# A four-stage attention and state-space model on one core: one activation table set, earlier reciprocals, moved norm products, and a two-lane final norm

## The chip, the cores and the metric

The kernel runs on one core of one Trainium2 chip. The metric is the device time of one execution in microseconds (us), lower is better. All data is float32.

## The reference, cut to what matters

The input is `x` of shape (8, 512, 256) and a context of shape (8, 64, 192). Four parts run one after the other, each adding to `x`:

```
L0: x += SelfAttn(LN(x));  x += CrossAttn(LN(x), ctx);  x += W2 (u * gelu(v)) with u, v = LN(x) Wp     (16 heads of 64)
L1: 64 context tokens in front of x, 4 mamba layers, each h += mamba(rmsnorm(h)); then rmsnorm(h); the 64 tokens dropped
L2: x += CrossAttn(LN(x), LN(ctx));  x += W2 gelu(LN(x) W1)                                            (16 heads of 16)
L3: x += one-head cross-attention with LN on both sides
LN(x) = (x - mean) * rsqrt(var + 1e-5) * g + b;      rmsnorm(x) = x * rsqrt(mean(x*x) + 1e-5) * w
attn = softmax(q k^T * scale) v
```

## The kernel before, in words

The kernel is written by hand, engine by engine. Each stage is a block with one instruction stream for each engine; semaphores order them, and a barrier stands between stages. `x` stays in SBUF as `X`, with the 256 features on partitions (two halves, KD = 2) and tokens along the free axis, so that the mean over features is a matmul with a matrix of 1/256. PSUM has 8 banks; bank 6 is `lane_v` (emptied by VectorE, the page's DVE), bank 7 is `lane_s` (emptied by ScalarE, ACT). The stages are self-attention, the first cross-attention, a gated feed-forward, a small prepend stage, mamba, `final_norm`, the second cross-attention (behind a norm of the context), a second feed-forward, and the last attention. Each loops over the 8 batches, and within batch b it prepares the norm of batch b+1.

**A layer norm** has these steps: TensorE (PE) makes the mean (L157), DVE subtracts it (`norm_centre_dve`, L174), ACT squares (L190), PE makes the variance in `lane_s` (`norm_variance_pe`, L166), ACT takes Ln in place (L197) and Exp with scale -0.5 (L199, which frees `lane_s`), together the reciprocal root (`norm_root_act`), DVE scales (L182) and ACT adds the bias (L206). ACT looks a function up in a table set; where the set held does not serve the function, the build puts an ACT_TABLE_LOAD in front. Before, Ln and Exp are served by two different sets.

**Self-attention** goes over 16 steps h; a step is a pair of heads with half of the queries, so two steps make one pair. A step has two units (u = 0, 1), each one tile of 128 queries for both heads. For each unit PE makes scores in two banks (L343), DVE takes the row maxima (L406), ACT exponentiates with row sums (L466), DVE inverts the sums (L412), POOL (GpSimd) multiplies the probabilities (L496), PE transposes them two steps later (L334, g = h - 2) into banks 4 and 5, which DVE (L401) and ACT (L458) copy out. These banks are single: the transposes of a unit wait for the copies of the unit before, the first half for DVE's, the second for ACT's. After every second step PE makes the output product (L360). The order in each stream is by hand: PE does transposes of (g,0), scores of (h,0), transposes of (g,1), scores of (h,1); DVE does copy (g,u), maximum (h,u), reciprocal (h-1,u); ACT does the copies of (g,0) and (g,1), then the exponentials of (h,0) and (h,1). The reciprocal is thus two units behind the maximum. Batches 0 to 6 carry the next batch's norm in this loop: PE's mean behind step g = 4, its variance behind g = 8, ACT's root (L478, L480) behind g = 9, DVE's scaling behind g = 10 and ACT's bias behind g = 12.

**Cross-attention** (`cross_attention`, used twice) goes over QT = 4 query tiles: PE makes the scores i = 0 to 3 (L676; from i = 2 on after DVE's subtraction i - 2 is done), then for t = 0 to 3 the transposes (L693), with the output projection of the batch before (`project_out`, L653, two parts) ahead of t = 0 and t = 2, then the mixing product (L703). `project_out` waits until both lanes are free. DVE does maximum (L765), subtraction (L767), sum (L774) and reciprocal (L776) of each tile, and POOL the multiplication (L621). The norm of the next batch stands in between: PE's mean behind score tile 1, its variance behind score tile 3; DVE's centring behind the sum of tile 0; ACT's squares behind exponential 2 and the root behind exponential 3.

**final_norm** (from L2078) is a loop over 8 batches with one lane: ACT squares, PE makes the mean square, ACT takes Sqrt, DVE a reciprocal over 512 columns (L2105) and two products (L2109).

## Time and profile before

| | us |
|---|---|
| median of 3 runs | 7805.58 (7801.66 to 7806.82) |
| the profiled execution's own time | 7797.73 |
| its span | 7795.7 |
| busy PE / DVE / ACT / POOL | 6613.3 / 5299.9 / 3872.3 / 4707.4 |

In the timeline a line is a run of like instructions: start, length, engine, source line, and in square brackets the idle time of that engine before it with what ended it. PEclk is the granted TensorE clock as a share of 2.4 GHz. A fp32 matmul or transposition stands as one or two instructions; "x16" counts instructions.

### The profile page before, as it was taken

Reading aid. Unit: us, or ns where it says so; the run is one execution under the profiler, and the core shown is the slowest. Engines: PE = TensorE matmul, PEld = TensorE weight load, DVE = VectorE, ACT = ScalarE, POOL = GpSimd, SP = SyncE. Lnnn points to the kernel's source line nnn. Section 1 sums busy time; section 2 is a strip of 40 time slices with the busy share of each in tenths; the row PEclk is TensorE's granted clock in tenths of the full one; section 3 lists DMA queues with packets and bytes.
Section 4 is the critical chain, followed back from the end, with each engine's and each line's share of the span. In section 5 each row is a group of like instructions: output and inputs, shape, how many; then the busy total and the mean of one; then the engine's idle time right before and its main releaser. Section 6 shows DMA issues by size and latency. Waiting matters only on the chain. (4 is left out here: it accounts for less than half of the span.)

```text
span 7795.7 us, 74709 instructions
## 1 busy us (share of the span) xinstructions
PE 6613.3 (85%) x20398; PEld 2699.1 (35%) x20398; DVE 5299.9 (68%) x6209; ACT 3872.3 (50%) x6998; POOL 4707.4 (60%) x2266
## 2 busy tenths in 40 slices
PE   7889898888898888888888888888888888777887
PEld 3444344444443323322333322332233332233333
DVE  3444444433321699999999999999999999755222
ACT  4444444322222566666666656666666666532332
POOL 2333333210000699999999999999999999611000
PEclk9999999988999999989999989999999998878998
DMA  1000000000000323323323332332332332300000
GB/s 65 0 0 0 0 0 0 17 0 0 15 0 2 78 61 83 76 70 87 80 69 70 90 75 69 82 77 61 93 80 61 84 79 68 85 5 0 0 0 22
DMA packets 205932, 351.49 MB, mean 45 GB/s; under 512 B 34112, under 2 KB 43008, under 8 KB 205360
## 3 DMA queue, kind: packets, MB, share of 16 engines
q1 hardware_dynamic: 205616, 347.96, 18.7%
q8 instruction: 115, 1.88, 0.1%
q14 instruction: 201, 1.65, 0.1%
HBM read 189.18 MB, written 6.62 MB: 25 GB/s over the span
## 5 line engine op out<-in xcount | busy, mean ns | idle before, releaser
L2046 POOL TENSOR_TENSOR work<-work,weights 128x1024 f32<-128x1024 f32 x1152 | 2691.4, 2361 | 19.1 <-DMA weights<-mamba_bc 12.8
L1903 PE MATMUL banks<-work 128*64 128x512 f32 x4608 | 1378.3, 680 | 629.0 <-POOL work L2051 615.6
L1965 DVE TENSOR_TENSOR_SCAN banks<-banks,work 128x512 f32<-128x512 f32 x1296 | 1617.7, 1270 | 70.8 <-ACT banks L2012 66.9
L2012 ACT ACTIVATE banks<-work 128x512 f32<-128x512 f32 x2304 | 1497.6, 680 | 67.0 <-DVE work L1729 43.2
L1965 DVE TENSOR_TENSOR_SCAN work<-banks,work 128x512 f32<-128x512 f32 x1008 | 1264.6, 1269 | 126.1 <-ACT banks L2012 79.4
L2051 POOL TENSOR_TENSOR work<-work,weights 128x1024 f32<-128x1024 f32 x504 | 1187.7, 2356 | 87.6 <-ACT work L1621 87.6
L1467 PE MATMUL banks<-work,weights 128*128 128x512 f32 (+31 forms) x3796 | 1164.1, 457 | 5.3 <-DVE work L1702 3.0
L496 POOL TENSOR_TENSOR work<-work 128x1024 f32<-128x1024 f32 x256 | 483.8, 1892 | 939.5 <-DVE work L412 939.5
L1467 PEld LDWEIGHTS banks<-work,weights 128*128 128x128 f32 x3796 | 643.8, 192 | 623.1 <-issue 543.7
L1747 DVE TENSOR_TENSOR work<-banks,weights 128x512 f32<-128x512 f32 x1296 | 852.8, 669 | 0.0
L1903 PEld LDWEIGHTS banks<-work 128*64 128x64 f32 x4608 | 267.0, 145 | 1502.8 <-POOL work L2051 920.5
L1625 ACT ACTIVATE work<-banks 128x2 f32<-128x2 f32 x648 | 111.4, 172 | 1217.6 <-DVE work L1747 1210.1
L406 DVE TENSOR_REDUCE work<-banks 128x2 f32<-128x1024 f32 x256 | 312.5, 1223 | 165.6 <-PE banks L343 165.4
L621 POOL TENSOR_TENSOR work<-work 128x1024 f32<-128x1024 f32 x64 | 121.0, 1900 | 440.1 <-DVE work L776 440.1
L466 ACT ACTIVATE work<-banks,work 128x512 f32<-128x512 f32 x512 | 346.1, 683 | 77.2 <-DVE work L406 77.2
L334 PE MATMUL banks<-ident,work 128*128 128x128 f32 x2048 | 284.9, 282 | 96.4 <-POOL work L496 81.2
L1485 PE MATMUL banks<-work,weights 128*128 128x512 f32 x592 | 351.3, 723 | 0.0
L889 PE MATMUL banks<-work,weights 128*128 128x512 f32 x768 | 341.8, 599 | 11.0 <-ACT work L206 11.0
L334 PEld LDWEIGHTS banks<-ident,work 128*128 128x128 f32 x2048 | 222.9, 142 | 290.1 <-POOL work L496 230.0
L343 PE MATMUL banks<-work 64*128 64x512 f32 x1024 | 294.2, 656 | 22.0 <-ACT work L466 16.4
L1050 POOL TENSOR_TENSOR work<-work,one 128x64 f32<-128x64 f32 (+1 forms) x16 | 4.3, 289 | 503.1 <-SPq L1044 312.7
L458 ACT ACTIVATE work<-banks 128x512 f32<-128x512 f32 x256 | 152.7, 596 | 237.3 <-PE banks L334 236.2
(218 smaller groups left out, 8418.8 us busy)
## 6 DMA issues: line engine op xcount, KB each, us to landing
weights<-mamba_bc SPq DMA_DIRECT2D x592, 256.0 KB, 5.0
work<-work SPq DMA_DIRECT2D x1160, 128.0 KB, 2.3
weights<-in_in_w SPq DMA_DIRECT2D x10, 512.0 KB, 4.1
weights<-in_conv_rows SPq DMA_DIRECT2D x20, 256.0 KB, 4.7
X<-in_xT SPq DMA_DIRECT2D x2, 2048.0 KB, 11.5
out_T<-X SPq DMA_DIRECT2D x2, 2048.0 KB, 9.7
weights<-in_out_w SPq DMA_DIRECT2D x5, 512.0 KB, 4.0
mamba_bc<-work SPq DMA_DIRECT2D x37, 64.0 KB, 1.6
```

The lines of the kernel that those rows point to most:

```text
L334: mm = e.transpose(core.banks[:, 4 + j, kt * P:(kt + 1) * P], probs[:, 2 * (g % 2) + u, j, kt * P:(kt + 1) * P], core.ident[:])
L466: last = e.activation(probs[:, slot, j, :], core.banks[:, 2 * u + j, :], ACT.Exp, bias=nmax[:, slot, j:j + 1], accum_out=sums[:, slot, j:j ...
L496: e.tensor_tensor(probs[:, slot], probs[:, slot], rsum[:, slot, :].unsqueeze(2).to_broadcast([P, 2, T]), ALU.mult) \
L889: mm = e.matmul(bank(i), w1[:, k, m * P:(m + 1) * P], normed[:, k, :], start=(k == 0), stop=(k == KD - 1))
L1467: mm = e.matmul(lane[:, a:b], conv_w[j][:, k, m * P:(m + 1) * P], nb[:, k, a + j:b + j], start=(d == 0 and k == 0), stop=(j == 0 and b == ...
L1485: mm = e.matmul(lane, z_w[:, k, m * P:(m + 1) * P], nb[:, k, TAPS - 1:], start=(k == 0), stop=(k == KD - 1))
L1747: last = e.tensor_tensor(ring_pair(n, j)[:, h, :], banks[:, slot_of(i), :], bc[:, j % SP_, 1, :], ALU.mult)
L1903: mm = e.matmul(ybank[k % 2][64 * h:64 * h + 64, :], fold, ring_pair(n, j)[:, h, :], start=False, stop=(a == SP_ - 1))
L1965: e.tensor_tensor_scan(ub if by_pool(j) else da, da, ub, state[:, i:i + 1], ALU.mult, ALU.add).then_inc(scanned, 1)
L2012: e.activation(banks[:, slot_of(i), :], dt_rep[:, k % 2, h, :], ACT.Exp, scale=decay[:, f:f + 1]).then_inc(da_full, 1)
L2046: e.tensor_tensor(ring_pair(n, j), u_rep[:, k % 2], bc[:, a, 0, :].unsqueeze(1).to_broadcast([P, 2, TC]), ALU.mult) \
L2051: e.tensor_tensor(ring_pair(n, q), ring_pair(n, q), bc[:, q % SP_, 1, :].unsqueeze(1).to_broadcast([P, 2, TC]), ALU.mult) \
```

## The change: what it does, and the diff

Five things. (1) At the start of ACT's stream in six stages and in the norm of the context, and before the root in the feed-forwards, the table set `natural_log_exp_and_others`, which holds both Ln and Exp, is loaded. (2) In self-attention DVE takes the reciprocal of the unit directly before the one whose maximum it has just made. (3) In the cross-attentions the mean and the centring go one tile forward, the squares go behind exponential 1, PE's variance goes behind the transposes of t = 0, and ACT's root behind the copy of t = 0. (4) `final_norm` uses the two lanes in turn and two buffers of squares, and takes Ln and Exp on ACT in place of Sqrt and DVE's reciprocal. (5) Its loops are written out.

```
@@ self_attention, vector
-                        if 0 < h <= H0:
-                            n = b * (H0 * UNITS) + ((h - 1) * UNITS + u)
-                            slot = 2 * ((h - 1) % 2) + u
-                            e.wait_ge(exp_done, n + 1)
+                        m = h * UNITS + u - 1
+                        if 0 <= m < H0 * UNITS:
+                            slot = m % (2 * UNITS)
+                            e.wait_ge(exp_done, b * (H0 * UNITS) + (m + 1))
                             e.reciprocal(rsum[:, slot, :], sums[:, slot, :]).then_inc(rsum_ready, 1)
@@ scalar, at the start: self_attention, norm_context, cross_attention, feed_forward, last_attention
+            e.preload_act_table_set("natural_log_exp_and_others")
@@ cross_attention, tensor
-                    if more and i == 1:
+                    if more and i == 0:
                         norm_mean_pe(e, core, ln, V, x_in(b + 1), core.mean_d, T)
-                    if more and i == 3:
-                        norm_variance_pe(e, core, nm, ln, S, b + 1, x_in(b + 1), core.mean_d, squared, T)
                 for t in range(QT):
...
                     mm.then_inc(t_full, 1)
+                    if more and t == 0:
+                        norm_variance_pe(e, core, nm, ln, S, b + 1, x_in(b + 1), core.mean_d, squared, T)
@@ cross_attention, vector
-                    if more and i == 1:
+                    if more and i == 0:
                         norm_centre_dve(e, core, ln, V, x_in(b + 1), centred, T)
@@ cross_attention, scalar
-                    if more and i == 2:
+                    if more and i == 1:
                         norm_square_act(e, nm, ln, v_done(b), rows, centred, squared)
-                    if more and i == 3:
-                        norm_root_act(e, core, nm, ln, S, b + 1, std, T)
                 for t in range(QT):
...
+                    if more and t == 0:
+                        norm_root_act(e, core, nm, ln, S, b + 1, std, T)
@@ feed_forward, scalar
                     if more and i == VARIANCE_AT:
+                        e.preload_act_table_set("natural_log_exp_and_others")
                         norm_root_act(e, core, nm, ln, S, b + 1, std, T)
@@ final_norm
+    squared, _ = core.area(0, 2, KD, T)
+    lane = lambda b: (core.lane_v, core.lane_s)[b % 2]
...
         @block.tensor
-            with e.Fori(0, B) as b:
+            for b in range(B):
                 e.wait_ge(squared_ready, b + 1)
-                e.wait_ge(s_free, b)
+                if b >= 2:
+                    e.wait_ge(scaled, b - 1)
                 for k in range(KD):
+                    mm = e.matmul(lane(b), core.mean_d[:], squared[:, b % 2, k, :], start=(k == 0), stop=(k == KD - 1))
...
         @block.scalar
+            e.preload_act_table_set("natural_log_exp_and_others")
+            for b in range(2):
+                e.activation(squared[:, b], x_in(b), ACT.Square).then_inc(squared_ready, 1)
+            for b in range(B):
+                e.wait_ge(full, b + 1)
+                e.activation(lane(b), lane(b), ACT.Ln, bias=core.eps[:]).then_inc(logged, 1)
+                if b + 2 < B:
+                    e.activation(squared[:, b % 2], x_in(b + 2), ACT.Square).then_inc(squared_ready, 1)
+                e.wait_ge(logged, b + 1)
+                e.activation(lane(b), lane(b), ACT.Exp, scale=-0.5).then_inc(rooted, 1)
...
         @block.vector
-                e.reciprocal(std, std).then_inc(inverted, 1)
+            for b in range(B):
+                e.wait_ge(rooted, b + 1)
                 for k in range(KD):
+                    last = e.scalar_tensor_tensor(out=x, in0=x, scalar=core.v("final", k), in1=lane(b), op0=ALU.mult, op1=ALU.mult)
                 last.then_inc(scaled, 1)
```

## Rows read from the trace of the kernel before

**Rows 1.** Windows: us, then each engine's busy time (instructions), PEclk, DMA share, GB/s
```profile
56.00:1447.00 1391.00, 1245.42 (x5157) 568.91 (x5155) 607.51 (x938) 621.92 (x1462) 483.84 (x256) 0.99 0.00 0
...
1447.00:2086.00 639.00, 558.64 (x1792) 292.79 (x1792) 239.65 (x300) 140.50 (x192) 69.53 (x67) 0.85 0.01 5
```

**Rows 2.** Groups of instructions on ACT: busy us, mean ns, idle before
```profile
L199 ACT ACT_TABLE_LOAD x43 | 55.2, 1283 | 0.8
...
L1688 ACT ACTIVATE banks<-banks,eps 128x512 f32<-128x512 f32 x38 | 25.2, 662 | 35.1 <-PE banks L1493 35.1
```

**Rows 3.** Timeline of two steps of self-attention: start us, us, engine, line
```profile
288.13 1.09 PE L334 MATMUL banks<-ident,work 128*128 128x128 f32 x8
...
293.07 0.21 ACT L466 ACTIVATION_READ_ACCUMULATOR work<-banks,work 128x1 f32 x1
...
293.66 1.09 PE L334 MATMUL banks<-ident,work 128*128 128x128 f32 x8 [1.29 <-POOL work L496]
...
295.01 0.59 ACT L458 ACTIVATE work<-banks 128x512 f32<-128x512 f32 x1
...
296.76 1.13 PE L343 MATMUL banks<-work 64*128 64x512 f32 x4
...
301.41 1.09 PE L334 MATMUL banks<-ident,work 128*128 128x128 f32 x8
```

**Rows 4.** Timeline of the two steps after the next batch's root
```profile
346.07 0.66 PE L334 MATMUL banks<-ident,work 128*128 128x128 f32 x4 [0.88 <-ACT work L458]
...
351.18 1.07 PE L334 MATMUL banks<-ident,work 128*128 128x128 f32 x8 [1.04 <-POOL work L496]
```

**Rows 5.** Timeline of the last batch of self-attention, first transposes
```profile
1327.05 1.09 PE L334 MATMUL banks<-ident,work 128*128 128x128 f32 x8 [1.63 <-POOL work L496]
```

**Rows 6.** Timeline of a batch of self-attention, last transposes
```profile
376.16 1.09 PE L334 MATMUL banks<-ident,work 128*128 128x128 f32 x8 [0.76 <-POOL work L496]
```

**Rows 7.** Timeline of one batch of the first cross-attention
```profile
1639.72 1.29 DVE L174 TENSOR_TENSOR work<-X,banks 128x512 f32<-128x512 f32 x2
...
1645.58 3.78 PE L166 MATMUL banks<-work,mean_d 128*128 128x512 f32 x4 [5.09 <-ACT work L190]
...
1652.17 9.49 PE L653 MATMUL banks<-work,weights 128*128 128x512 f32 x16 [2.81 <-ACT work L199]
```

**Rows 8.** Windows: scores to mixing, of batches with and without a norm
```profile
1631.36:1672.90 41.54, 32.76 (x137) 19.59 (x137) 20.46 (x24) 11.48 (x14) 7.56 (x4) 0.84 0.00 0
...
2034.30:2061.81 27.51, 25.41 (x128) 16.81 (x129) 18.78 (x22) 6.61 (x8) 7.57 (x4) 1.00 0.00 1
...
7014.51:7045.00 30.49, 21.59 (x65) 10.82 (x65) 20.47 (x24) 11.48 (x14) 7.56 (x4) 0.83 0.00 0
...
7202.73:7226.78 24.05, 17.28 (x56) 8.70 (x57) 18.77 (x22) 6.39 (x8) 7.56 (x4) 0.86 0.00 0
```

**Rows 9.** Timeline of the last batch of the second cross-attention
```profile
7220.50 3.75 PE L653 MATMUL banks<-work,weights 128*128 128x512 f32 x4 [2.15 <-DVE X L750]
```

**Rows 10.** Window of the whole final norm, columns as in Rows 1
```profile
6779.00:6840.00 61.00, 29.45 (x32) 9.05 (x32) 37.88 (x24) 34.48 (x32) 0.00 (x0) 0.54 0.15 49
```

**Rows 11.** Timeline of one batch of the final norm
```profile
6793.21 3.35 DVE L2105 RECIPROCAL work<-work 128x512 f32<-128x512 f32 x1 [2.09 <-ACT work L2099]
...
6794.49 1.06 ACT L2096 ACTIVATE work<-X 128x1024 f32 x1
...
6795.60 3.78 PE L2089 MATMUL banks<-work,mean_d 128*128 128x512 f32 x4 [3.26 <-ACT work L2096]
...
6796.72 1.42 DVE L2109 SCALAR_TENSOR_TENSOR X<-X,vec,work 128x512 f32 x2 [0.16 <-DVE work L2105]
```

**Rows 12.** Timeline of the first feed-forward's first norm
```profile
2094.92 1.28 ACT L199 ACT_TABLE_LOAD   x1
...
2096.22 0.60 ACT L199 ACTIVATE work<-banks 128x512 f32<-128x512 f32 x1
...
2099.68 9.31 PE L889 MATMUL banks<-work,weights 128*128 128x512 f32 x16 [5.47 <-ACT work L206]
```

More of the change, by code:

```diff
@@ L942, in _ @@
             V, S = Count(), Count()
+            e.preload_act_table_set("natural_log_exp_and_others")
             norm_act(e, core, nm, ln, V, S, 0, rows, centred, squared, std, normed, norm[1], T)
@@ L953, in body @@
                     if more and i == VARIANCE_AT:
+                        e.preload_act_table_set("natural_log_exp_and_others")
                         norm_root_act(e, core, nm, ln, S, b + 1, std, T)
@@ L1179, in _ @@
             V, S = Count(), Count()
+            e.preload_act_table_set("natural_log_exp_and_others")
             norm_act(e, core, nm, ln, V, S, 0, rows, centred, squared, std, normed, "beq", T)
@@ L2071, in final_norm @@
 def final_norm(core):
-    squared, at = core.area(0, KD, T)
-    std, at = core.area(at, T)
-    s_full, s_free = core.sem("final_s_full"), core.sem("final_s_free")
-    squared_ready, inverted = core.sem("final_squared"), core.sem("final_inverted")
-    scaled = core.sem("final_scaled")
+    squared, _ = core.area(0, 2, KD, T)
+    full, logged, rooted = core.sem("final_full"), core.sem("final_logged"), core.sem("final_rooted")
+    squared_ready, scaled = core.sem("final_squared"), core.sem("final_scaled")
+    lane = lambda b: (core.lane_v, core.lane_s)[b % 2]
+    x_in = lambda b: core.X[:, :, b, PRE:S1]
     with core.nc.Block() as block:
@@ L2084, in _ @@
         def _(e):
-            with e.Fori(0, B) as b:
+            for b in range(B):
                 e.wait_ge(squared_ready, b + 1)
-                e.wait_ge(s_free, b)
+                if b >= 2:
+                    e.wait_ge(scaled, b - 1)
                 for k in range(KD):
-                    mm = e.matmul(core.lane_s, core.mean_d[:], squared[:, k, :], start=(k == 0), stop=(k == KD - 1))
-                mm.then_inc(s_full, 1)
+                    mm = e.matmul(lane(b), core.mean_d[:], squared[:, b % 2, k, :], start=(k == 0), stop=(k == KD - 1))
+                mm.then_inc(full, 1)
         @block.scalar
         def _(e):
-            with e.Fori(0, B) as b:
-                e.wait_ge(s_full, b)
-                e.activation(squared, core.X[:, :, b, PRE:S1], ACT.Square).then_inc(squared_ready, 1)
-                e.wait_ge(s_full, b + 1)
-                e.wait_ge(scaled, b)
-                e.activation(std, core.lane_s, ACT.Sqrt, bias=core.eps[:]).then_inc(s_free, 1)
+            e.preload_act_table_set("natural_log_exp_and_others")
+            for b in range(2):
[7 more added lines that the diff above has]
+                e.activation(lane(b), lane(b), ACT.Exp, scale=-0.5).then_inc(rooted, 1)
         @block.vector
         def _(e):
-            with e.Fori(0, B) as b:
-                e.wait_ge(s_free, b + 1)
-                e.reciprocal(std, std).then_inc(inverted, 1)
-                e.wait_ge(inverted, b + 1)
+            for b in range(B):
+                e.wait_ge(rooted, b + 1)
                 for k in range(KD):
                     x = core.X[:, k, b, PRE:S1]
-                    last = e.scalar_tensor_tensor(out=x, in0=x, scalar=core.v("final", k), in1=std, op0=ALU.mult, op1=ALU.mult)
+                    last = e.scalar_tensor_tensor(out=x, in0=x, scalar=core.v("final", k), in1=lane(b), op0=ALU.mult, op1=ALU.mult)
                 last.then_inc(scaled, 1)
```

## The prediction

> **What bounds the kernel now.** I read first the windows by stage, because the change leaves the mamba stage alone. In self-attention PE is busy 1245 of 1391 us with a granted clock of 0.99; in the first cross-attention it is busy 559 of 639 us at only 0.85 [rows 1]. No other engine is near its share, so PE sets the end of these stages and each stretch in which it waits is time. The groups on ACT come next: the load of the set for Exp at L199 stands 43 times, 1283 ns each; mamba's Ln at L1688 runs 38 times at 662 ns, and no load stands at its line, since its stage loads the joint set by hand [rows 2]. Then I read the timelines stage by stage for what ends PE's waits.
>
> **Self-attention.** Two steps take 301.41 - 288.13 = 13.28 us, with one gap in PE: the transposes at 293.66 waited 1.29 us for POOL [rows 3], whose multiplication had waited for a reciprocal that stood behind a maximum it does not need. One unit earlier, this reciprocal comes 2 us sooner and the POOL wait goes. What is late next is ACT: the second half of the following transposes needs ACT's copy of this unit, which stands behind the exponentials and starts at 295.01 however early the transposes are, since nothing ahead of it moves. It ends at 295.60; the half takes 0.6, so scores start at 296.25 and not at 296.76 [rows 3]. A plain pair of steps gains 0.5 us; the bounds are 0 (ACT takes all) and 1.29 (the whole gap), and I take 0.5, because the copy's start is read from the trace. The reciprocal now also waits for the exponential just issued; behind it in DVE's queue stand the copy and the next maximum, for which PE and ACT wait. The exponential of the first unit ends at 293.07 + 0.21 = 293.28, just ahead of the 293.66 by which maximum, reciprocal and copy turn over [rows 3], so this costs nothing; if ACT came later it would.
> Batches 0 to 6 have in this loop two plain pairs of steps (1.0), three in which the norm's mean, variance or bias already fills the gap (0), and the pair after the root. There ACT's two loads held a copy back (PE waits 0.88) and POOL held the next transposes (1.04) [rows 4]; DVE's scaling still stands ahead of a copy, and I take 1.1 of the 1.9. At the start the first transposes waited 1.63 for POOL [rows 5]; with the first 0.5 I take 2.1. At the end the last transposes waited 0.76 [rows 6], as those before them did in like manner, and then DVE's copies space them: 0.9. Sum 5.1 a batch, times 7, and for batch 7 without norm 6 x 0.5 + 2.1 + 0.9 = 6.0: **42 us**. Bounds: start and end alone, 24; the whole 1.29 in each plain pair (20 pairs), 58.
>
> **First cross-attention.** In a batch with a norm PE waits 5.09 us for ACT's squares ahead of the variance and 2.81 us for the root ahead of the projection, and after these waits both run at the lower clock, 3.78 and 9.49 us [rows 7]. The whole stretch from scores to mixing is 41.54 us at a granted clock of 0.84. Batch 7, with the same work less the two norm products, has 27.51 us at 1.00 [rows 8]. In the new order the projection's first part stands where the squares were waited for, the squares come one tile sooner, and the variance stands behind one set of transposes, so I take batch 7's stretch plus two products of 3.78 / 2: 31.3 us. The fourth score tile will wait about 1 us for DVE, as the centring (1.29 [rows 7]) now precedes the second maximum; batch 7 has such waits too. The second part of the projection waits for the root, which stands behind ACT's copy: variance end, Ln 0.66, Exp 0.6, against one set of transposes, some 0.6 us. What is queued behind the root on ACT is the copy of t = 1, needed only two transposes later. The gain is 10.2 a batch. It is had by batches 1 to 6; batch 0 has no projection to fill with, and DVE and POOL bound it as before. **61 us**. If the lower clock stayed in the variance and projection, (9.49 + 3.78) / 2 = 6.6 less a batch would leave 22; if the 0.6 vanished it would be 65.
>
> **Second cross-attention.** The same stretch takes 30.49 us, in batch 7 24.05 [rows 8]. Here the projection is short and DVE's chain of maxima and sums sets the pace, so the centring's 1.29 adds: 25.3, a gain of 5.1. In batch 7 the projection's second part waited 2.15 us for DVE and ran at half clock, 3.75 [rows 9]; the variance fills part of the wait, and at full clock 1.9 more would be gained. I take 6 between 5.1 and 7.0, times 6: **36 us**.
>
> **Final norm.** It takes 61.0 us at a granted clock of 0.54, near 1.2 GHz [rows 10]. Each batch chains table loads, reciprocal 3.35 and products 1.42 [rows 11]. With two lanes, batch b+2 waits for b: matmul 3.78, Ln 0.66 [rows 2], Square 1.06 of the batch after next, Exp 0.6 (as the ACT copy in [rows 3]), products 1.42 [rows 11], with hops 7.6 for two batches. The whole is 2.4 (load, square) + 3.6 + 3 x 7.6 + 3.8 + 2.7 (Ln, Exp, products) = 35.3: **26 us**. If PE went to 2.4 GHz, matmuls of 1.9 would give 26.4 and a gain of 35. I take the first, because in this stage PE still waits about half the time.
>
> **Entries.** Each stage's first norm has the load for Exp on the path (1.28 at 2094.92, and the first product waits 5.47 for the chain [rows 12]); the load for Ln hides behind the variance and the new one behind the mean. Where the context's projection covers the norm, nothing is gained. Left are self-attention, the two feed-forwards and the two context norms: 5 x 1.28 = **6 us**. In the feed-forward loops ACT's loads hide under PE's products, and the last attention's under its variance: 0; were that cover gone, each load would be 1.28.
>
> **A rule against the row.** The load starts at 2094.92 and its Exp at 2096.22, 1.30 us later [rows 12]. The Trainium skill (ScalarE: Activation LUTs, What ACT_TABLE_LOAD costs) gives a switch of set 2.66 us, with a drain beside the 1283 ns. By that the entries would give 13 us and the whole 7 more; the trace shows no such drain, and I keep the row.
>
> **The sum** is 42 + 61 + 36 + 26 + 6 = 171 us. Against the profiled execution (span 7795.7, own time 7797.73) that is 7627; the median of the runs lies 7.9 above it, so I forecast 7634.
>
> **Rivals.** (A) The lower clock stays. Where small waits remain, PE falls back to 1.2 GHz, as it did in [rows 9]; the first cross-attention then gives 22 to 45: about 7660. For it speaks that row, against it batch 7's 1.00 in [rows 8]. Chance 0.12.
> (B) More overlap: self-attention gets its whole gap (58) and the final norm rises to the full clock (35), so 196: 7609. Against it stands the copy at 295.01. Chance 0.15. The Trainium skill (TensorE: Matmul & The Clock Gate, What's actually happening) has the clock low by default and raised by activity, which is the final norm's half of this rival; 0.54 in [rows 10] agrees for the sparse stage.
> (C) The loads don't go. Where the set differs between a loop's entry and its end, the build might load again at every root. Then entries 6 and the root's 1.1 x 7 are lost, the root's 2.6 longer wait stands ahead of the projection in 12 batches (31), and the final norm gets two loads in its chain (15): 171 - 60 = 111, 7695. Mamba's Ln without a load [rows 2] speaks against it. Chance 0.05.
> (D) Slower. The reciprocal, one unit behind, waits for ACT in every unit, and the copy and maximum behind it on DVE hold up PE. To undo 171 us and cost 16 more over 256 units it needs 0.73 us each; it decides from where the exponential ends that much after DVE's maximum. In [rows 3] it ends before. With 0.8 us each the time would be about 7840. Chance 0.03.
>
> **How the numbers follow.** The forecast has 0.65. All ends at once on the low side are 24 + 22 + 31 + 25 + 6 = 108 and on the high side 58 + 65 + 42 + 35 + 6 = 206; they won't coincide, so I give 7595 to 7675, which holds A and B and leaves out C and D. A measurement of this kernel can tell about 0.2%, 16 us, from no change. All cases but D are faster by more; a mixture of D with the rest could end near zero: faster 0.95, same 0.02, slower 0.03.
>
> **What would show it.** Right: no load at L197, L199, L478 and L480; self-attention's POOL waits ahead of L334 nearly gone, replaced by waits for L458, with 12.8 us for a plain pair of steps; the first cross-attention's stretch near 31 us at a clock near 1.00; the second's near 25; the final norm near 35. Wrong: PE waits for L401 with DVE waiting for L466 at L412; variances or projections at 3.8 and 9.5 us; loads that stay.

## The result, and the profile after

The changed kernel takes **7623.39 us** (median of 4 runs, 7616.94 to 7624.9); the kernel before took 7806.2 us (median of 4, 7801.66 to 7812.9). The ratio is 0.9764 with a 95% interval of 0.9747 to 0.978: faster, and 10.6 us under the forecast of 7634. The profiled execution of the changed kernel is the 7616.94 one, with a span of 7615.0 us; that of before has 7795.7, so the two profiles differ by 180.7 us. All comparisons of stages below are between profiled executions.

First come the windows of the four stages that the change touches, in the order self-attention, first cross-attention, final norm, second cross-attention: us, each engine's busy time, PEclk, DMA share, GB/s.

```profile
28.42:1404.61 1376.19, 1263.54 (x5184) 572.92 (x5185) 609.74 (x945) 608.93 (x1458) 484.37 (x257) 0.99 0.01 2
1404.61:1981.55 576.94, 536.94 (x1793) 285.97 (x1793) 237.60 (x299) 120.62 (x178) 69.38 (x67) 0.88 0.02 6
6672.74:6700.77 28.03, 16.89 (x33) 6.16 (x33) 11.24 (x16) 18.25 (x26) 0.00 (x0) 0.94 0.32 108
6714.98:7063.23 348.25, 278.82 (x801) 137.52 (x801) 202.97 (x249) 89.58 (x130) 70.42 (x67) 0.92 0.01 3
```

Cut at the same instructions (the first product of each stage; for the final norm its first instruction on ACT), the whole span divides like this. The forecast's 6 us of entries stand in the stages where they fall.

| stage | before, us | after, us | gain | forecast |
|---|---|---|---|---|
| self-attention | 1419.4 | 1376.2 | 43.2 | 42 + 1.3 |
| first cross-attention | 638.2 | 576.9 | 61.3 | 61 |
| first feed-forward, context tokens | 425.8 | 425.5 | 0.3 | 1.3 |
| mamba | 4267.4 | 4265.7 | 1.7 | 0 |
| final norm | 61.4 | 28.0 | 33.4 | 26 |
| second context norm | 16.6 | 14.2 | 2.4 | 1.3 |
| second cross-attention | 383.6 | 348.3 | 35.3 | 36 |
| second feed-forward | 281.0 | 281.1 | -0.1 | 1.3 |
| last context norm, last attention | 274.0 | 270.6 | 3.3 | 1.3 |
| sum | | | 180.8 | 171.5 |

The waits of PE over self-attention say what took the place of what (us in total, times, longest). Before, the wait of L334 for POOL stood first among them with 81.2 us in 76 times.

```profile
PE banks L334 <- ACT work L459: 29.5, 36, 1.8
...
PE banks L334 <- DVE work L401: 12.7, 31, 0.5
PE banks L334 <- POOL work L497: 8.9, 7, 1.3
```

Next come two steps on PE's timeline. The first fence is the pair that answers to [rows 3] (batch 1); the second is the pair in which ACT adds the norm's bias (batch 0), and under it two rows of the same pair in batch 1:

```profile
278.37 1.09 PE L334 MATMUL banks<-ident,work 128*128 128x128 f32 x8
...
285.89 0.66 PE L334 MATMUL banks<-ident,work 128*128 128x128 f32 x4 [0.59 <-ACT work L459]
...
291.12 1.09 PE L334 MATMUL banks<-ident,work 128*128 128x128 f32 x8
```

```profile
173.68 1.09 PE L334 MATMUL banks<-ident,work 128*128 128x128 f32 x8
...
182.43 1.05 PE L334 MATMUL banks<-ident,work 128*128 128x128 f32 x4 [1.80 <-ACT work L459]
183.41 2.08 PE L343 MATMUL banks<-work 64*128 64x512 f32 x4
...
189.25 0.98 PE L334 MATMUL banks<-ident,work 128*128 128x128 f32 x7
...
353.62 0.66 PE L334 MATMUL banks<-ident,work 128*128 128x128 f32 x4 [1.81 <-ACT work L459]
354.20 1.13 PE L343 MATMUL banks<-work 64*128 64x512 f32 x4
```

On ACT, in that second pair of batch 0, the copy that PE waits for stands behind the bias:

```profile
180.56 1.32 ACT L486 ACTIVATE work<-work,vec 128x512 f32<-128x512 f32 x2
181.79 0.59 ACT L459 ACTIVATE work<-banks 128x512 f32<-128x512 f32 x1
```

The plain pair takes 291.12 - 278.37 = 12.75 us and the 1.29 us for POOL are gone. The pair with the bias takes 15.57 us in batch 0, where it took 13.98. In batch 1 it takes 13.98 as before, with the same wait for ACT: there the scores behind the wait run at the full clock (1.13 us), and in batch 0 at the lower one (2.08).

The answer to [rows 7] and [rows 8] is a batch of the first cross-attention on PE: scores, projection, transposes, variance, second part of the projection, mixing.

```profile
1588.10 2.05 PE L678 MATMUL banks<-work 128*128 128x128 f32 x16 [0.87 <-DVE work L769]
1589.99 7.03 PE L655 MATMUL banks<-work,weights 128*128 128x512 f32 x16
1596.86 1.04 PE L693 MATMUL banks<-ident,work 128*128 128x128 f32 x8
1597.73 1.88 PE L166 MATMUL banks<-work,mean_d 128*128 128x512 f32 x4
...
1600.99 7.13 PE L655 MATMUL banks<-work,weights 128*128 128x512 f32 x16 [0.51 <-ACT work L199]
```

The waits of 5.09 and 2.81 us have become none and 0.51. The variance takes 1.88 us in place of 3.78 and the projection 7.13 in place of 9.49, both at the full clock. The same windows as in [rows 8], from scores to mixing, of the first and the second cross-attention:

```profile
1579.89:1610.78 30.89, 28.61 (x137) 18.23 (x137) 20.22 (x24) 8.81 (x12) 7.56 (x4) 1.00 0.00 0
6818.21:6843.72 25.51, 19.92 (x65) 10.39 (x65) 20.14 (x24) 8.58 (x12) 7.56 (x4) 0.93 0.00 0
```

The final norm's timeline, one round of two batches, answers to [rows 11]:

```profile
6682.32 3.98 PE L2096 MATMUL banks<-work,mean_d 128*128 128x512 f32 x8 [2.02 <-ACT work L2108]
...
6684.31 0.66 ACT L2106 ACTIVATE banks<-banks,eps 128x512 f32<-128x512 f32 x1 [1.55 <-PE banks L2096]
...
6684.90 1.05 ACT L2108 ACTIVATE work<-X 128x1024 f32<-128x1024 f32 x1
...
6685.84 0.59 ACT L2110 ACTIVATE banks<-banks 128x512 f32<-128x512 f32 x1
...
6686.46 1.41 DVE L2118 SCALAR_TENSOR_TENSOR X<-X,vec,banks 128x512 f32<-128x512 f32 x2 [2.26 <-ACT banks L2110]
...
6688.01 3.98 PE L2096 MATMUL banks<-work,mean_d 128*128 128x512 f32 x8 [1.71 <-ACT work L2108]
```

Two batches now take 6688.01 - 6682.32 = 5.69 us, at a granted clock of 0.94 in the stage where it was 0.54 [rows 10]. The view puts PE's wait down to a Square of ACT, but the Square that the first product at 6688.01 needs is the one that ended at 6685.95. What ended just before is DVE's pair of products (6686.46 + 1.41 = 6687.87), for which the code makes PE wait too; this is the chain that the prediction added up.

How a round of the kernel before was closed matters for the experiments below. [rows 11] has its reciprocal and products, and one more row shows what followed them on ACT:

```profile
6798.22 1.28 ACT L2099 ACT_TABLE_LOAD   x1 [2.67 <-DVE X L2109]
```

A batch there takes 7.02 us: load 1.28, Sqrt 0.69, reciprocal 3.35, products 1.42 and small hops. Sqrt took its result out of the lane into SBUF, so PE's product of the next batch ran beside the reciprocal and DVE's products (6795.60 + 3.78 = 6799.38 [rows 11], just ahead of the next Sqrt at 6799.51) and was not in this chain.

### The profile page after: what moved, and what is told of

The parts are those of the page before. It is cut to its first block and busy times, and to the rows that moved or that the text cites. A ratio compares the mean times of both kernels' runs of the same rounds, so it can differ in the third digit from the quotient of the medians.

```text
span 7615.0 us, 74498 instructions
## 1 busy us (share of the span) xinstructions
PE 6568.7 (86%) x20398; PEld 2686.0 (35%) x20398; DVE 5267.6 (69%) x6201; ACT 3751.5 (49%) x6912; POOL 4707.9 (62%) x2266
## 3 DMA queue, kind: packets, MB, share of 16 engines
q8 instruction: 115, 1.88, 0.1%
## 5 line engine op out<-in xcount | busy, mean ns | idle before, releaser
L1473 PEld LDWEIGHTS banks<-work,weights 128*128 128x128 f32 x3796 | 644.5, 192 | 623.6 <-issue 544.0
L334 PE MATMUL banks<-ident,work 128*128 128x128 f32 x2048 | 286.3, 279 | 51.9 <-ACT work L459 29.5
L334 PEld LDWEIGHTS banks<-ident,work 128*128 128x128 f32 x2048 | 220.1, 141 | 245.5 <-POOL work L497 106.4
```

Source lines behind the costliest of these rows:

```text
L334: mm = e.transpose(core.banks[:, 4 + j, kt * P:(kt + 1) * P], probs[:, 2 * (g % 2) + u, j, kt * P:(kt + 1) * P], core.ident[:])
L1473: mm = e.matmul(lane[:, a:b], conv_w[j][:, k, m * P:(m + 1) * P], nb[:, k, a + j:b + j], start=(d == 0 and k == 0), stop=(j == 0 and b == ...
```

## The experiments

Theory at the start: each part works where the prediction put it, and self-attention is now held by ACT's copy. Each run undoes or moves one part of the changed kernel. A time given without a range is of a single run; its span is set against the changed kernel's span of 7615.0, and the stage concerned against the table above. Stages with the same code differ between the runs of this study: self-attention 1376.2 to 1378.8 us, the first cross-attention 576.7 to 581.2, the second 347.9 to 355.5. A difference of stages below these spreads says little unless its rows are shown.

**Loads back.** All hand-made loads outside mamba are taken out, so that the build places its own.

```
-            e.preload_act_table_set("natural_log_exp_and_others")   (7 places)
```

> The changed kernel without the loads of the joint set by hand (outside mamba); all places stay new, so that the build puts a load ahead of each Ln and each Exp again. Theory (the set is a small part, felt where ACT stands ahead of PE): the root of the first cross-attention is 2.6 us longer, and the wait for it ahead of the projection's second part grows from 0.5 to about 3.1 us in 6 batches, with the lower clock behind it (16 to 35 us in all); the second cross-attention hides it behind DVE's residual, 0 to 6; self-attention loses 3.5 at its entry and 1 to 2 a batch behind the root (11 to 17); the final norm loses two loads in a batch on two lanes (12 to 25); other entries 5. Time 7670 to 7710. Rival (the new places hide the loads, the set was worth its entries alone): 7623 to 7640. Rival (the set is the whole gain): above 7750.

7637.28 us, span 7635.3: 20 more. The groups of table loads on ACT, and one root of the first cross-attention on ACT, with the second part of the projection that waits for it on PE:

```profile
L197 ACT ACT_TABLE_LOAD x33 | 42.3, 1283 | 0.6
L199 ACT ACT_TABLE_LOAD x33 | 42.3, 1283 | 0.6
```

```profile
1606.58 1.28 ACT L197 ACT_TABLE_LOAD   x1
1607.88 0.66 ACT L197 ACTIVATE banks<-banks,eps 128x512 f32<-128x512 f32 x1
1608.56 1.28 ACT L199 ACT_TABLE_LOAD   x1
```

```profile
1610.50 7.13 PE L653 MATMUL banks<-work,weights 128*128 128x512 f32 x16 [1.98 <-ACT work L199]
```

The expected 7670 to 7710 did not come; the time lies in the rival's 7623 to 7640. The loads are back at the roots of self-attention, the first cross-attention, the feed-forwards and the last stage, and yet the price is 11.5 us in the first cross-attention and 4.8 in self-attention. The load for Ln runs while PE still makes the variance; only the one for Exp shows, and PE's wait rises by 1.98 - 0.51 = 1.47 us in each of six batches. The projection behind it stays at 7.13. In self-attention the entry is 3.7 us longer, and the pair behind each root takes 14.37 us again for 13.27; but in this run all seven pairs with the bias take 13.98, where four of the changed kernel's ran partly at the lower clock, and so a batch is hardly longer (170.9 us for 170.7). With the new places, then, the loads cost little. The Trainium skill (ScalarE: Activation LUTs, What ACT_TABLE_LOAD costs) gives a switch of set 2.66 us; the row's load at 1608.56 is followed by its Exp 1.29 us later, and the pair of loads adds 1.47 to PE's wait, so the measurement decides against that figure. The run did not test the loads everywhere, though. In the final norm, the second context norm and the second cross-attention no load came back (none stands in its trace there); mamba loads the joint set by hand ahead of them.

**Reciprocals back to two units behind.**

```
-                        m = h * UNITS + u - 1
-                        if 0 <= m < H0 * UNITS:
+                        if 0 < h <= H0:
+                            slot = 2 * ((h - 1) % 2) + u
```

> The changed kernel with the reciprocal of self-attention two units behind, as before. Theory: a plain pair of steps goes from 12.76 back to 13.27 us, PE waits 1.29 for POOL in it, and the loop's gain is lost but for what the table set gives behind the root: self-attention 30 to 38 us longer, 7655 to 7663. Rival (ACT is the limit and the table set made the gain): less than 10 us longer, below 7635.

7669.9 us; self-attention 1418.0 in place of 1376.2. The waits of PE in that stage:

```profile
PE banks L334 <- POOL work L497: 78.3, 69, 1.7
```

POOL's 8.9 us are 78.3 again, and the stage is 41.8 us longer, more than the 30 to 38 expected; the total is 7 above its range as well. Nearly all that self-attention gained is this one reciprocal. The joint set alone gives 1419.4 - 1418.0 = 1.4 us while POOL holds PE, and 4.8 once it does not (the run before); the stage's spread is 2.6. The pair behind the root takes 13.32 us here, where it took 14.37 before: what that pair gained is the joint set's, and not the reciprocal's.

**Cross-attention's norm at its old places, with the joint set kept.**

```
-                    if more and i == 0:
+                    if more and i == 1:
                         norm_mean_pe(...)
+                    if more and i == 3:
+                        norm_variance_pe(...)
...
-                    if more and t == 0:
-                        norm_variance_pe(...)
```

(and centring, squares and root on DVE and ACT in like manner)

> The changed kernel with the old places of mean, centring, squares, variance and root in both cross-attentions, the joint set kept. Theory: waits for the squares (5.1 us) come back in full, the wait for the root falls from 2.8 to about 0.3 us since two loads are gone, and some of the slow clock behind it with it: of the 61 and 35 us gained, 18 to 30 and 15 to 20 stay, so 46 to 63 come back: 7669 to 7686. Rival (the places are the whole gain, the set adds nothing): 96 come back, 7720.

7687.68 us, span 7685.7: 70.7 more, 1.7 us above the range expected. The stages are 623.6 and 365.8 us, so the places are worth 46.7 in the first cross-attention and 17.5 in the second; the rest of the gains, 14.6 and 17.8, is the joint set at the old places (in the second within the spread of 7 us). PE's waits in the first (the window runs on into the feed-forward, which has one of the nine waits for L190):

```profile
PE banks L166 <- ACT work L190: 41.0, 9, 5.1
PE banks L655 <- ACT work L199: 8.3, 6, 1.4
```

The wait for the root was expected to fall to 0.3 us and is 1.4. Before, PE waited for it 17.3 us over the stage, so the joint set took 9.0 of them away; in the run without loads by hand the same wait rose from 3.0 to 11.9, by 8.9. The loads thus cost PE the same at the old places and at the new. The stage's 14.6 for 11.5 differ by less than its spread.

**Final norm over one lane**, with Ln and Exp kept.

```
-    lane = lambda b: (core.lane_v, core.lane_s)[b % 2]
+    lane = lambda b: core.lane_s
...
-                if b >= 2:
-                    e.wait_ge(scaled, b - 1)
+                if b >= 1:
+                    e.wait_ge(scaled, b)
```

> The changed kernel with one lane in the final norm: the matmul of a batch waits for the products of the batch before; two buffers of squares, Ln and Exp stay. Theory (the second lane makes the gain): a batch chains matmul, Ln 0.66, Square 1.05, Exp 0.6 and products 1.4 with hops, 5.9 us at 2.4 GHz and 7.8 at 1.2 GHz, against 7.0 before: the stage takes 50 to 65 us and not 28, and the whole 7645 to 7660. Rival (Ln and Exp in place of loads and reciprocal make it): the stage stays below 40 us, 7635 or less.

7650.46 us. The window of the stage, columns as above, and two rows of its timeline:

```profile
6673.76:6733.20 59.44, 28.62 (x32) 8.93 (x33) 11.25 (x16) 18.52 (x26) 0.00 (x0) 0.59 0.15 51
```

```profile
6682.42 3.75 PE L2096 MATMUL banks<-work,mean_d 128*128 128x512 f32 x4 [3.74 <-DVE X L2118]
...
6689.92 3.75 PE L2096 MATMUL banks<-work,mean_d 128*128 128x512 f32 x4 [3.74 <-DVE X L2118]
```

The stage is 59.4 us, hardly less than the 61.4 of before, although it has neither the long reciprocal nor the 16 loads: with one lane, 3.75 of products at half clock and 3.74 of waiting fill 7.50 a batch. Against the changed kernel the second lane is thus worth 31.4 us, the higher granted clock that comes with it included. Against the kernel before, this run is no clean comparison: there PE's product ran beside the reciprocal, and here it must wait until DVE has used the lane, so PE's product has come into the chain.

**Final norm over two lanes, with Sqrt and the reciprocal.** The load by hand of this stage is taken out too.

```
-                e.activation(lane(b), lane(b), ACT.Ln, bias=core.eps[:]).then_inc(logged, 1)
+                e.activation(lane(b), lane(b), ACT.Sqrt, bias=core.eps[:]).then_inc(rooted, 1)
...
+                e.reciprocal(lane(b), lane(b)).then_inc(logged, 1)
```

> The changed kernel, its final norm with two lanes kept but with Sqrt on ScalarE and the reciprocal of 512 columns on VectorE in place of Ln and Exp. If the second lane is what pays and the reciprocal was merely exposed: VectorE is the bound with 3.35 + 1.41 + some 0.4 us a batch, the stage 42 to 46 us in place of 28, the total 7637 to 7643. Rival, the reciprocal is hidden by the second lane: 28 to 32 us, 7623 to 7627. Rival, two lanes give nothing without the logarithm: 59 us as with one lane, 7655.

7646.77 us. The stage and two rounds on DVE:

```profile
6676.13:6718.30 42.17, 21.22 (x33) 7.02 (x33) 37.55 (x24) 14.34 (x18) 0.00 (x0) 0.75 0.21 72
```

```profile
6689.59 3.36 DVE L2113 RECIPROCAL banks<-banks 128x512 f32<-128x512 f32 x1
...
6694.31 3.36 DVE L2113 RECIPROCAL banks<-banks 128x512 f32<-128x512 f32 x1
```

The stage takes 42.2 us, just inside the 42 to 46 of the first theory. DVE is busy 37.55 of them and a batch takes 6694.31 - 6689.59 = 4.72: DVE is the bound, as that theory had it. Ln and Exp are thus worth 14.1 us once there are two lanes (42.2 to 28.0). What brings 61.4 down to 42.2 is not the lanes alone: this run also has the second buffer of squares and the written-out loop, and in its trace a single load stands in the stage, where the kernel before had 16, one of them (1.28 us) in each batch's chain of 7.02. If only that load left the chain in eight batches, it would be some 10 of the 19 us, an estimate from these rows; no run keeps the loads with two lanes, so the share of each stays open. The total came out 3.8 us above the range expected. That part is not the final norm: the second cross-attention, whose code this run leaves alone, took 355.5 us at a granted clock of 0.89, where the changed kernel had 348.25 at 0.92.

**ACT's copy ahead.** In steps of odd g, ACT copies the first unit's half ahead of the second unit's exponential, and no longer behind it.

```
+                            if u == 1 and g + 1 > 0 and early(g + 1):
+                                copy_out(g + 1, 0)
                             (the exponential of unit u)
```

> A version beyond the change, self-attention alone: in odd steps ACT's copy of the first unit stands ahead of the second exponential of the step before (not behind steps 4 and 8 in batches with a norm). Theory (ACT's copy behind the exponentials is what now holds the transposes): the waits for it (0.59 us) go, a plain pair of steps falls from 12.76 to 11.9 to 12.1 us, and the pair with the bias loses its 1.8 us: 25 to 40 us less, 7585 to 7600. Rival (the exponential comes late and holds the scores of two steps on): the wait turns into one for L467 and the time is 7615 to 7640.

7597.18 us; self-attention is 1345.6 in place of 1376.2. The pair of steps that answers to 278.37 above:

```profile
274.02 1.09 PE L334 MATMUL banks<-ident,work 128*128 128x128 f32 x8
...
280.33 1.06 PE L334 MATMUL banks<-ident,work 128*128 128x128 f32 x8
...
285.98 1.09 PE L334 MATMUL banks<-ident,work 128*128 128x128 f32 x8
```

The transposes at 280.33 come in one piece, without a wait, and the pair takes 11.96 us. Of the 29.5 us that L334 waited for ACT's copy, 1.1 are left. Moving that copy alone gives 30.6 us, so the prediction's "What is late next is ACT" is shown. Time and stage are in the ranges expected, and the pair with the bias takes 12.79 us in all seven batches.

**Residual sum early, in the second cross-attention.** PE's projection there waited 2.78 us for DVE's residual sum at L752; the sum goes ahead of the scores of group 3.

```
+                    if earlier and i == RESIDUAL_AT:     (3 where tiles is 2)
+                        residual(b - 1, 0)
```

> A version beyond the change, second cross-attention alone: DVE's first residual product stands ahead of the maximum of tile 3 and not behind the last reciprocal. Theory: PE's wait of 2.8 us for it ahead of the projection's second part shrinks to the root's, 2 us, and the projection runs at the full clock; DVE's chain is 0.7 longer: the stretch of 25.5 to 26.4 us falls by 1 to 2.5, in 7 batches 7 to 17 us, 7606 to 7616. Rival (the chain of sums and POOL's last product is the limit): no change or 5 us more, 7621 to 7628.

7624.04 us, the stage 348.2: nothing gained, as the rival's 7621 to 7628 had it. PE in the same place of a batch:

```profile
6847.39 2.69 PE L656 MATMUL banks<-work,weights 128*128 128x512 f32 x4 [2.73 <-ACT work L199]
```

The wait has the same length and another releaser: the root, which stands behind an exponential and a copy. Batch 7, which has no root to make, did gain: from scores to mixing it takes 22.18 us for 24.21. Together with the copy ahead, in four runs:

> Both versions beyond the change together. Theory: the gains lie in different stages and add: 7570 to 7592, ratio to the kernel before 0.970 to 0.973. Rival (either brings nothing): 7600 to 7625.

7592.18 us (7588.87 to 7595.97, 4 runs), ratio 0.974 (0.9724 to 0.9756) to before, both just outside what was expected. Nearly all of it is the copy.

**Only variance and root moved.** In cross-attention the mean, the centring and the squares go back to their old places; variance and root stay where the change put them.

```
-                    if more and i == 0:
+                    if more and i == 1:
                         norm_mean_pe(...)          (the centring likewise, squares at i == 2)
```

> The changed kernel, in which mean and centring stand one tile later and the squares behind exponential 2, as before; variance and root stay in their new places. Theory: with the projection in front of the variance the squares are in time anyway, so moving mean and centring earlier is worth nothing, and the fourth score tile no longer waits 0.9 us for DVE: the stretch of the first cross-attention 30.0 to 30.9 us, of the second 26 to 27; time 7617 to 7627. Rival (the squares one tile sooner are needed): PE waits for L190 ahead of the variance, 2 us or more in 12 batches, 7650 or more.

7610.06 us, span 7608.1: 6.9 less, and 7 us below the range expected. The stages are 571.9 and 344.9 us, 5.0 and 3.4 less than the changed kernel's; both lie below every run of this study with mean, centring and squares forward and the rest alike. Where the fourth group's scores waited 0.87 us for DVE above, they run on here:

```profile
1581.84 3.73 PE L678 MATMUL banks<-work 128*128 128x128 f32 x32
1586.14 7.13 PE L655 MATMUL banks<-work,weights 128*128 128x512 f32 x16 [0.57 <-DVE work L174]
```

Part of that wait comes back ahead of the projection, and the stretch from scores to mixing is 30.56 us for 30.89. In the second cross-attention the stretch is 23.96 for 25.51, but there the query projection took some 5.4 us in six of eight batches, where it takes 3.70 in six of the changed kernel's: what the order gave, the lower clock took back, and only the 3.4 are left.

**The best of both.** First the copy ahead and the old places for mean, centring and squares in one kernel. Then the same, but in the second cross-attention with mean, centring and squares where the change put them, the root ahead of exponential 3 and the residual sum early.

```
+                    if more and i == ROOT_AT:            (3 where tiles is 2)
+                        norm_root_act(...)
                     e.wait_ge(shifted, b * QT + (i + 1))
```

> The changed kernel with two edits of earlier runs together: the copy of odd steps ahead of the second exponential (alone 7597), and in cross-attention the mean products, the centring and the squares back at their places of before, the variance and the root where the change put them (alone 7610). The stages are apart, so the gains should add: 26 + 13 = 39 us under the changed kernel, 7582 to 7588. Rival: both gains are partly the same granted clock or a difference of chips, and the two together give no more than the copy alone, 7592 to 7600.

7582.15 us (7580.09 to 7590.88, 4 runs), ratio 0.9729 (0.9712 to 0.9745) to before: 41 us under the changed kernel's median, and the gains add as expected. The stages are 1345.6, 573.2 and 345.0 us, together 37.6 less than in the changed kernel. Of the 41, some may be the chip's: the kernel before took 7793.35 us beside this run and 7806.2 beside the changed kernel, and by the ratios (0.9729 and 0.9764) the gain is nearer to 27.

> As x9, and in the second cross-attention alone the centring and squares where the change put them, the first residual sum ahead of the scores of group 3, and ScalarE's root ahead of exponential 3. In the run with the residual early TensorE waited 2.73 us for the root, which stood behind exponential 3 and copy 0. If that order alone held it: a batch of the second part is 1.5 to 2.7 us shorter on seven batches, 7570 to 7578. Rival: VectorE is the bound there by now (reductions, differences, sums and copies without a gap), and the wait only moves to its copies ahead of the value products: 7582 to 7588, as x9.

7587.97 us (7585.47 to 7594.15, 4 runs), the second cross-attention 344.9: no gain over the run before it, and the time is the rival's. The root's new place did give something: the run with the residual early alone has the same code there but for the root, and its stage is 348.2, its stretches 25.5 to 26.8 us for 23.6 to 24.5 here. DVE in that place:

```profile
6802.62 1.21 DVE L779 TENSOR_REDUCE work<-banks 128x16 f32<-128x1024 f32 x1
6803.87 1.22 DVE L781 TENSOR_TENSOR work<-banks,work 128x1024 f32<-128x1024 f32 x1
6805.01 1.21 DVE L788 TENSOR_REDUCE work<-work 128x16 f32<-128x1024 f32 x1
6806.25 0.25 DVE L790 RECIPROCAL work<-work 128x16 f32<-128x16 f32 x1
6806.42 1.16 DVE L788 TENSOR_REDUCE work<-work 128x16 f32<-128x1024 f32 x1
```

and PE's longest sum of waits in the stage:

```profile
PE banks L703 <- POOL work L633: 28.6, 24, 2.7
```

No row of DVE shows an idle time. PE's waits for the root and, but for one, for the residual are gone, and PE waits instead for POOL, which waits for DVE's sums. In this stretch DVE is now the bound; with the root ahead of exponential 3 the order on ACT no longer is.

## Why the prediction was right

The forecast of 7634 and the range of 7595 to 7675 held, with a miss of 10.6 us. Its terms were right in mechanism and most in size; two sums came out right in part by luck, as errors in them cancelled.

**Self-attention: 43.2 for 42 + 1.3, by parts that miss in both directions.** The plain pair gained 0.53 for 0.5 (13.28 to 12.75), and by what was named: the wait for POOL turned into a wait for ACT's copy [rows 3]. The pair after the root takes 173.68 - 160.42 = 13.26 us and took 14.37, 1.11 for 1.1, with POOL's wait of 1.27 still there behind DVE's scaling; with the reciprocals two units behind it takes 13.32, so nearly all of this is the joint set's. From one batch's first scores to the next takes (1281.05 - 86.16) / 7 = 170.7 us, and took 175.5: 4.8 for 5.1. The last batch gained 6.2 for 6.0. Two terms were wrong in size. The start was taken at 2.1 and gave 3.36 in batch 1 (from its first scores to the second pair's first transposes, 23.30 to 19.94); over batches 0 to 6 it gave 1.6 to 4.9, 2.7 on the mean. The pair with the bias was put at 0, "already fills the gap". That holds for three of seven batches, which take 13.98 as before. In the other four it lost 1.6: not by the wait for ACT at its bias, which is 1.8 us with or without the loss, but because the work behind the wait ran at the lower clock (2.08 us for 1.13). On the mean it lost 0.9, which outweighs the 0.6 that the start gave beyond its term. The run with the copy ahead shows that the wait was ACT's order: without it no such pair falls to the lower clock, and the batches take (1255.79 - 86.85) / 7 = 167.0 us. The run with reciprocals two units behind shows that the reciprocal's place carries 41.8 of the stage.

**First cross-attention: 61.3 for 61.** The stretch is 30.89 us for 31.3, at a clock of 1.00; the wait for the root 0.51 for 0.6; the fourth scores wait 0.87 for 1. Rival (A), the clock that stays low, did not come. Right in sum, the term left open what part did it; the runs divide it in 46.7 for places and 14.6 for the set. They also show that three of the five moved steps (mean, centring, squares) bring nothing: with them at their old places the stage is 5.0 us shorter (3.7 in a second run), and its variance still does not wait. The prediction had that cost in it as "The fourth score tile will wait about 1 us", but not that it bought nothing.

**Second cross-attention: 35.3 for 36, the sum partly by luck.** The stretch is 25.51 for 25.3 in most batches, and over batches 1 to 6 it gave 28 us for 31 (6 x 5.1). The other 5 of the forecast were to come from the projection at the full clock, the 1.9 of batch 7 [rows 9]. They did not: there are 2.78 us of waiting and 2.74 for products that take 1.9. In their place some 6 us came from where the sum had nothing: the query projection (L668) takes 3.70 us in six of eight batches, where six of the eight took 5.2 to 6.4 before (L666). DVE's chain sets the pace, as the term said and the last run shows.

**Final norm: 33.4 for 26, the largest miss.** The step that failed is "I take the first, because in this stage PE still waits about half the time": matmuls of 3.78 in the chain of a round. With both lanes' products back to back PE was granted 0.94, a batch's products take half of 3.98 us, and a round 5.69 in place of 7.6, which is this one term's 1.9 less; this is the final norm's half of rival (B), priced at 35. The run with one lane, in which PE waits half the time in pieces of 3.74 us, stayed at 0.59. The Trainium skill (TensorE: Matmul & The Clock Gate, What's actually happening) has the clock raised by activity; the traces agree with 0.59 and 0.94. The chain was right; its one mis-sized term is the product, 3.78 taken and 2.0 measured.

**Entries: 6 forecast, and some 10 come at the entries (3.4, 2.9, 2.4 and 1.3), of which 4.0 are given back behind them.** The second context norm gave 2.4 for 1.3. Self-attention's entry gave 3.4 instead of 1.3: the trace of before has a load ahead of the first Square too (at 33.75), which the prediction overlooked, and the variance ran in 2.90 us in place of 3.75. In the first feed-forward the first product of the projection comes 10.75 us into the stage, where it came 13.61 in, but behind it 0.9 went to a slower first product and 1.7 to slower ones ahead of mamba, at a lower granted clock (0.70 for 0.76, and 0.55 for 0.61). In the second feed-forward PE's wait is 4.2 for 5.5, and the stage is no shorter. The last stage's 3.3 and mamba's 1.7 are not assigned to the change: over the runs of this study the last stage took from 270 to 281 us with the same code.

**Rivals.** (C), loads that stay, was priced at 60 us. The loads did go. Its price was tried only in part by the first run, where no load came back in the final norm (priced 15) and the second cross-attention (half of 31). Where loads did come back, the price was too high, but not by far: 1.47 us a batch for 2.6 in the first cross-attention, since with the new places one load of each pair lies under PE's product; 1.1 behind each root of self-attention, as priced, though the bias pairs, all at the full clock in that run, gave most of it back. What the run costs is 20 us in all. (D), reciprocals that wait for ACT, did not come: PE's waits for DVE at L334 rose from 5.6 to 12.7 us over the stage, none longer than 0.5.

What stays open: how much of the second cross-attention's 17.8 us for the joint set is load time and how much is clock, why the granted clock of identical stages differs between runs, and how the final norm's first 19 us divide between the second lane, the second buffer, the written-out loop and the 15 loads that went. The written-out loops were not tried alone in any run.

## What to carry to other kernels

When a wait of the bounding engine is removed, the order of work on the engine that is late next decides how much is kept: here one reciprocal gave 42 us, and one copy ahead of one exponential another 31. Of a change that moves several steps at once, undo each by itself: three moved steps of cross-attention brought nothing, and the stages are 8 us (5.0 + 3.4) shorter without them. In a chain of small steps a second buffer was worth 31 us on top of the cheaper steps, and the cheaper steps 14 on top of the second buffer; and a run that undoes one part must be read for what else left the chain with it, as the loads did here. Where a pair of steps takes longer though its waits do not, look at the clock of the work behind them.

## What the runs showed of the hardware that was not expected

- A table load beside a product of TensorE was nearly free: 1.47 us of each pair of 1283 ns showed in the first cross-attention. In the run without loads by hand none came back in the three stages behind mamba, which had loaded the joint set by hand.
- The final norm's granted clock was 0.54 before and 0.94 in the changed kernel; it was 0.75 with two lanes and a wait for VectorE between the products, and 0.59 with one lane.
- The same code of the second cross-attention took 348.25 us at a granted clock of 0.92 in one run and 355.5 at 0.89 in another. One profile of one stage of this kernel can't tell less than some 7 us from nothing, unless the clock is read beside it.
- The same wait of 1.8 us of TensorE was followed by scores at the full clock in one batch of self-attention (1.13 us) and at the lower one in another (2.08).
